# A graph network of four parts on one core: slots of nodes by a scatter beside the node network, out-degrees counted beside the attention

## The chip, the core and the metric

One of the eight cores of a Trainium2 chip runs the whole program in one launch. The metric is the device time in microseconds from start to end of an execution. A core has TensorE (PE, with weight loads PEld), VectorE (DVE), ScalarE (ACT), GpSimd (POOL) and SyncE (SP); SP and GpSimd issue transfers, and 16 DMA engines carry them out.

## The reference, cut to what matters

The input is x (50000 nodes x 128), and 25000 edges (src, dst) sorted by dst. Four networks follow one another, each wrapped as `x = layernorm(x + network(x))`: SAGE with three layers (mean over incoming edges), an attention network with two attention layers and a mean, a network (below "jk") with four layers, and a GCN with three layers.

```python
# the third network: where the degrees are used
deg_out = segment_sum(ones, src, num_segments=n)
deg_in = segment_sum(ones, dst, num_segments=n)
norm_src = rsqrt(maximum(deg_out, 1.0))
norm_dst = rsqrt(maximum(deg_in, 1.0))
for i in range(N_LAYERS):
    m = h * norm_src
    agg = segment_sum(m[src], dst, num_segments=n)
    h = agg * norm_dst
    ...
```

All four networks read `h[src]`, the present value of an edge's source node.

## The kernel before

**Slots.** Only a node that is the dst of some edge gets messages. The edges, padded to 25088 (`SLOTS`), lie as slots in 49 groups (`EG`) of 512, four sub-tiles of 128 each, 196 sub-tiles (`ET`) in all. The last slot of a run of equal dst holds that node's values; other slots hold partial sums. All 50176 (`NODES_PAD`) nodes, 98 groups (`NG`) of 512, are also computed as if they had no incoming edge. A DRAM table holds slots first and the lonely nodes behind, so an edge's source is either "slot s" or "`SLOTS` + node". This number per edge is the `idx` of every later gather. `goes_on` is a mask of bytes, one per slot: same dst as the slot before. `node_mask` marks the nodes without a slot. `l2_weight` is norm_src times norm_dst per edge.

**Blocks.** The program is a row of blocks; each ends with the wait for its stores, and a barrier of all engines. In order: setup; the node network of SAGE (`node_net_block`, here sage_nodes); `maps_block`; sage0 (`slot_hidden_block`), `meta_block`, sage1, `sage_end_block`; `fetch_block`; softmax1, gat1 (`attend_block`), ln1, second, softmax2, gat2, ln2; `mean_block`; `jk_start_block`, four jk layers, jk_end; the node network of the GCN, and three blocks of its slots. Inside a block each engine has its own program; `run_groups` steps over the groups and calls stages with a lag each, in the order of the list, and `wait_for` waits for a semaphore of a group. That order is fixed when the kernel is built; there is no planner.

**Node network of SAGE.** For 98 groups, SP loads x (line 813), TensorE turns it and runs three layers, ScalarE copies and applies ReLU, VectorE adds x and normalizes (lines 700 to 717, 1023 to 1056), SP stores h1, h2, x2 and u. Beside it, GpSimd gathers for the 49 edge groups the x rows of src and dst (`stash`, line 615, 2 x 196 indirect transfers of 128 rows) and writes them to tables of their own (`put`, line 882). At the end GpSimd zeroes `x_in` and `x_again` (lines 888 and 890) for the last, partial group, which SP waits for.

**maps_block.** SP loads dst of each group, repeated over the partitions (`near`, line 527). VectorE compares it with itself shifted by one (`goes_on`, line 573). For each of 196 sub-tiles VectorE makes five one-hot tiles in bf16 (lines 582 to 586): low nine bits and high bits of src and dst, the last two times the slot's tile number and place. TensorE adds three products of them up in PSUM over all sub-tiles (line 554): the count of edges per source, and tile and place of the last slot per destination. VectorE combines these into two numbers a node (out-degree, place), stored as the DRAM table `meta`, and `node_mask` is made.

**sage0 and meta_block.** In sage0 the first SAGE layer of the slots is computed from the stashed rows; beside it, GpSimd gathers the two numbers of `meta` for the source of every edge (`SmallGather`, a ring of five buffers, VectorE copies each into `src_meta`). meta_block makes `idx`, `idx_y`, `idx_jk` and `l2_weight` of them (lines 668 to 676).

**fetch, softmax, gat.** fetch_block is only 196 gathers of GpSimd (line 644). A softmax block is a chain of short operations of VectorE, with TensorE and ScalarE between. In gat, ScalarE weights the fetched rows, VectorE scans and adds (lines 1559 to 1570), GpSimd scales each group's own rows (line 1520).

**Indirect transfers.** GpSimd's transfers are indirect ones: one instruction takes 128 row numbers from a column in SBUF.

The functions that the diff touches:

## Time and profile before

| | us |
|---|---|
| runs shown: median (lowest, highest) | 7210.41 (7204.28, 7210.70) |
| the profiled execution's own time | 7209.73 |
| its span, first to last instruction | 7207.8 |
| PE / PEld / DVE / ACT / POOL busy | 5032.8 / 3367.5 / 4784.7 / 3062.6 / 3388.1 |
| maps_block, first transfer to the next block's first | 1104.96 to 1373.91 |

The mean granted clock of TensorE is 0.801 of its full 2.4 GHz. "Busy" is the time in which an engine had an instruction under way; an idle time is shown in brackets with what ended it. A share near 1 of one engine in a stretch says that this engine sets the pace there. A DMA share of 1 means that all 16 engines had packets under way.

### The profile page before, as it was taken

Reading aid. Unit: us, or ns where it says so; the run is one execution under the profiler, and the core shown is the slowest. Engines: PE = TensorE matmul, PEld = TensorE weight load, DVE = VectorE, ACT = ScalarE, POOL = GpSimd, SP = SyncE. Lnnn points to the kernel's source line nnn. Section 1 sums busy time; section 2 is a strip of 40 time slices with the busy share of each in tenths; the row PEclk is TensorE's granted clock in tenths of the full one; section 3 lists DMA queues with packets and bytes.
Section 4 is the critical chain, followed back from the end, with each engine's and each line's share of the span. In section 5 each row is a group of like instructions: output and inputs, shape, how many; then the busy total and the mean of one; then the engine's idle time right before and its main releaser. Section 6 shows DMA issues by size and latency. Waiting matters only on the chain. (4 is left out here: it accounts for less than half of the span.)

```text
span 7207.8 us, 88239 instructions
## 1 busy us (share of the span) xinstructions
PE 5032.8 (70%) x24324; PEld 3367.5 (47%) x24324; DVE 4784.7 (66%) x14503; ACT 3062.6 (42%) x6979; POOL 3388.1 (47%) x3407
## 2 busy tenths in 40 slices
PE   7999995798989920697435555444489998679221
PEld 5777771364558810596323232221156665456111
DVE  5888789733347612888885566677878886655454
ACT  4666660263333300654444444336756554346000
POOL 5666000274434454373567666673300001765677
PEclk9999999999998955597557667665589999889555
DMA  5888551496766621696445698757856665766332
GB/s 194 277 276 277 214 198 61 126 305 226 245 205 203 195 67 35 175 350 212 140 137 148 129 136 131 122 100 219 270 197 222 222 223 199 209 203 194 95 93 82
DMA packets 1093011, 1317.61 MB, mean 183 GB/s; under 512 B 110351, under 2 KB 791999, under 8 KB 1086254
## 3 DMA queue, kind: packets, MB, share of 16 engines
q1 hardware_dynamic: 974926, 1058.13, 44.3%
q0 software_dynamic: 117600, 253.84, 17.3%
q8 instruction: 203, 3.33, 0.2%
q14 instruction: 282, 2.31, 0.1%
HBM read 633.42 MB, written 682.00 MB: 183 GB/s over the span
## 5 line engine op out<-in xcount | busy, mean ns | idle before, releaser
L615 POOL DMA_INDIRECT jk_layer_msg<-jk,idx_jk x588 | 591.5, 1006 | 268.2 <-issue 174.0
L615 POOL DMA_INDIRECT gcn_msg<-x,idx x196 | 186.9, 954 | 898.0 <-POOLq L137 838.6
L1148 PE MATMUL jk_layer_sum_ps<-ident,jk_layer_weighted 128*128 128x128 f32 x784 | 185.5, 380 | 540.5 <-ACT jk_layer_weighted L1114 540.5
L1148 PEld LDWEIGHTS jk_layer_sum_ps<-ident,jk_layer_weighted 128*128 128x128 f32 x784 | 118.6, 188 | 660.2 <-ACT jk_layer_weighted L1114 660.2
L742 PE MATMUL gcn_nodes_h_ps<-gcn_nodes_h_t,w_gcn 128*128 128x512 f32 x784 | 352.7, 593 | 0.0
L742 PE MATMUL sage_nodes_h_ps<-sage_nodes_h_t,w_ws 128*128 128x512 f32 x784 | 352.5, 592 | 0.0
L1282 DVE COPY sage_h<-sage_turn 128x512 f32<-128x512 f32 x98 | 67.7, 691 | 417.3 <-PE sage_turn L733 417.3
L615 POOL DMA_INDIRECT sage_small_rows<-meta,src_node x196 | 185.0, 944 | 324.2 <-POOLq L137 264.8
L962 ACT ACTIVATE sage_nodes_h_t<-sage_nodes_h_ps,w_b_c 128x512 f32<-128x512 f32 x392 | 247.8, 683 | 198.8 <-PE sage_nodes_h_ps L742 198.8
L2185 PE MATMUL gcn_end_sum_ps<-ident,gcn_end_rows 128*128 128x128 f32 x196 | 54.6, 434 | 389.4 <-DVE gcn_end_rows L2178 389.4
L615 POOL DMA_INDIRECT sage_end_msg<-h,idx x196 | 197.0, 1005 | 270.2 <-ACT sage_end_weighted L1114 159.5
L742 PE MATMUL jk_layer_h_ps<-jk_layer_sum_t,w_jk_w 128*128 128x512 f32 x392 | 321.3, 916 | 0.8 <-DVE jk_layer_sum_t L1170 0.6
L1170 DVE TENSOR_TENSOR_SCAN jk_layer_sum_t<-goes_on,jk_layer_sum_t,jk_layer_sum_ps 128x512 f32<-128x512 uint8 x196 | 249.8, 1274 | 90.2 <-PE jk_layer_sum_ps L1148 90.2
L1950 ACT ACTIVATE jk_layer_h_t<-jk_layer_h_ps,w_jk_b 128x512 f32<-128x512 f32 x196 | 134.7, 687 | 401.9 <-PE jk_layer_h_ps L742 350.0
L962 ACT ACTIVATE gcn_nodes_h_t<-gcn_nodes_h_ps,w_gcn_b_c 128x512 f32<-128x512 f32 x392 | 245.9, 677 | 122.5 <-PE gcn_nodes_h_ps L742 122.5
L1114 ACT ACTIVATE sage_weighted<-sage_msg,inv_deg 128x128 f32<-128x128 f32 (+1 forms) x392 | 146.5, 451 | 353.9 <-DMA sage_msg<-x_msg 336.7
L615 POOL DMA_INDIRECT sage_msg<-h,idx x196 | 185.3, 945 | 230.0 <-ACT sage_weighted L1114 152.2
L742 PE MATMUL sage_h_ps<-sage_sum_t,w_wn 128*128 128x512 f32 x588 | 287.5, 598 | 2.1 <-issue 2.1
L742 PE MATMUL sage_h_ps<-sage_own_t,w_ws 128*128 128x512 f32 x588 | 284.4, 592 | 0.0
L615 POOL DMA_INDIRECT sage_nodes_fetched<-in_x,src_x x196 | 201.5, 1028 | 109.1 <-issue 59.5
L1263 ACT ACTIVATE sage_h_t<-sage_h_ps,w_b_c 128x512 f32<-128x512 f32 x196 | 124.1, 684 | 292.7 <-PE sage_h_ps L742 292.5
L615 POOL DMA_INDIRECT gcn_msg<-r,idx x196 | 201.7, 1029 | 96.6 <-issue 55.4
(481 smaller groups left out, 15979.2 us busy)
## 6 DMA issues: line engine op xcount, KB each, us to landing
h<-sage_nodes_h SPq DMA_DIRECT2D x196, 512.0 KB
h_t<-sage_h_t SPq DMA_DIRECT2D x98, 512.0 KB
h<-sage_h SPq DMA_DIRECT2D x98, 512.0 KB, 3.6
jk_t<-jk_layer_h_t SPq DMA_DIRECT2D x196, 256.0 KB
jk_end_layers<-jk_t SPq DMA_DIRECT2D x49, 1024.0 KB, 5.3
r<-gcn_nodes_h SPq DMA_DIRECT2D x98, 512.0 KB
second_x_in<-u SPq DMA_DIRECT2D x147, 260.0 KB
jk<-jk_layer_h SPq DMA_DIRECT2D x147, 256.0 KB, 4.5
```

The costliest lines, as they stand in the source:

```text
L615: pool.indirect_dma_start(out=into[:, g.number % depth, s, :], out_offset=None, in_=table, in_offset=bass.IndirectOffsetOnAxis(ap=index_ti ...
L742: mm = pe.matmul(ps[:, c, :], w[:, k, c * P:(c + 1) * P], x[:, k, :], start=n == 0, stop=n == len(terms) - 1)
L962: ins = act.activation(tile[:, g.b, c, :], ps[:, c, :], ACT.Relu, bias=bias[:, c:c + 1])
L1114: ins = act.activation(self.weighted[:, g.b, s, :], self.rows_of(g)[:, s, :], self.func, scale=self.weights[0][:, cols(g, SUB, s, 1)])
L1148: mm = pe.transpose(ps[:, c, at_s], self.weighted[:, g.b, s, c * P:(c + 1) * P], self.K.ident[:])
L1170: dve.tensor_tensor_scan(self.sum_t[:, g.b, c, :], self.K.goes_on[:, cols(g, GROUP)], self.ps[g.b][:, c, :], self.sum_t[:, 1 - g.b, c, GRO ...
L1263: ins = act.activation(h_t[:, g.b, c, :], h_ps[:, c, :], ACT.Relu, bias=bias[:, c:c + 1])
L1282: dve.tensor_copy(h[:, g.b, 2:4, :], turn_ps[1][:]).then_inc(out_b.sem, 1)
L1950: act.activation(h_t[:, g.b, 0, :], h_ps[g.b][:, 0, :], ACT.Relu, bias=W.jk_b[:, i:i + 1]).then_inc(kept.sem, 1)
L2185: mm = pe.transpose(self.ps[g.b][:, c, s * P:(s + 1) * P], self.rows[:, g.b, s, c * P:(c + 1) * P], self.K.ident[:])
```

## The change

**Place of a node by a scatter.** maps_block is gone. In setup GpSimd makes `slot_no` (slot s of partition p and sub-tile t: 128 t + p). In the node network of SAGE GpSimd first makes the default places `SLOTS` + node (an iota), SP stores them as the DRAM table `place` before its first load, and after the stash GpSimd issues 196 indirect scatters of one 4-byte number per partition, slot number to row dst, where `idx_out` sends every slot that is not the last of its run out of bounds. GpSimd waits for all of them before it zeroes `x_in` and `x_again`. The `near` loads are in SP's stages of the node network (lag 6), the masks in VectorE's (lag 7), for the first 49 groups. In sage0 GpSimd gathers `place` for each source straight into `K.place`, without a ring and without copies on VectorE. `places_block` takes the place of meta_block: it makes the index tiles and, from a load of the whole table with four numbers a piece, `node_mask`.

**Out-degrees.** `SourceCounts` makes the one-hot tiles of src in fetch_block, two compares and one matmul per sub-tile, and stores the counts. `CountFetch` gathers the count of each edge's source: 42 sub-tiles in softmax1, 66 in gat1, 20 in softmax2, 68 in gat2. `l2_weight` is made in jk_start_block. Five weight tensors (`lin`, three of the GCN, `jk_w`) are loaded in mean_block and not in setup; setup no longer turns dst's high and low parts.

```diff
 # setup: gpsimd
+        link(pool.iota(iota_i[:], pattern=[[1, GROUP]], base=-RJ, channel_multiplier=0))
+        link(pool.tensor_copy(K.lo_iota[:], iota_i[:]))
...
+        link(pool.iota(K.slot_no[:], pattern=[[P, ET]], base=0, channel_multiplier=1))
 # setup: vector
-        for who, tile in (("src", src_i), ("dst", dst_i)):
-            dve.tensor_single_scalar(hi_i[:], tile[:], 9, op=ALU.logical_shift_right)
...
+        dve.tensor_single_scalar(hi_i[:], src_i[:], 9, op=ALU.logical_shift_right)
...
-def maps_block(nc, K, tables):
...
+class SourceCounts:
+    def __init__(self, ph, K, table):
+        self.lo_hot, self.hi_hot = ph.sb("lo_hot", [P, 2, GROUP], BF16), ph.sb("hi_hot", [P, 2, P], BF16)
...
+    def vector_hot(self, dve, t):
+        wait_for(dve, self.hot_used, Group(t - 2))
+        dve.tensor_scalar(self.lo_hot[:, t % 2, :], self.K.lo_iota[:], self.K.src_lo[:, t:t + 1], None, ALU.is_equal)
+        dve.tensor_scalar(self.hi_hot[:, t % 2, :], self.K.hi_iota[:], self.K.src_hi[:, t:t + 1], None, ALU.is_equal).then_inc(self.hot_ready.sem, 1)
+    def tensor_count(self, pe, t):
+        wait_for(pe, self.hot_ready, Group(t))
+        pe.matmul(self.ps[:], self.hi_hot[:, t % 2, :], self.lo_hot[:, t % 2, :], start=t == 0, stop=t == ET - 1).then_inc(self.hot_used.sem, 1)
...
+class CountFetch:
+    def pool_part(self, pool, step=0, steps=1):
+        n = self.end - self.first
+        for t in range(self.first + n * step // steps, self.first + n * (step + 1) // steps):
+            pool.indirect_dma_start(out=self.K.src_count[:, t:t + 1], out_offset=None, in_=self.table,
+                                    in_offset=bass.IndirectOffsetOnAxis(ap=self.K.src_node[:, t:t + 1], axis=0)).then_inc(self.arrived, 16)
+    def pool_wait(self, pool):
+        pool.wait_ge(self.arrived, 16 * (self.end - self.first))
...
 # fetch_block
+        for t in range(ET):
+            counts.vector_hot(dve, t)
+        counts.vector_keep(dve)
...
 # places_block, in place of meta_block
+            sp.dma_start(node_place[:], tables["place"].rearrange("(g p s) k -> p g (s k)", p=P, s=SUB)).then_inc(loaded, 16)
...
+        dve.wait_ge(loaded, 16)
+        link(dve.tensor_copy(node_where[:], node_place[:]))
+        link(dve.tensor_scalar(K.node_mask[:], node_where[:], float(SLOTS), None, ALU.is_ge))
+        link(dve.scalar_tensor_tensor(K.node_mask[:], node_where[:], float(SLOTS + N_NODES), K.node_mask[:], ALU.is_lt, ALU.mult))
...
 # node network of SAGE: sync
+            sp.wait_ge(nodes_ready, 1)
+            sp.dma_start(tables["place"].rearrange("(p c) k -> p (c k)", p=P), node_no[:]).then_inc(places_set, 16)
+            stages = [(load, -1), (load_near, 6), (reload, 3), (store_h1, 3), (store_h2, 4), (store_u, 7), (store_y, 6)]
 # gpsimd
+            pool.iota(node_no[:], pattern=[[1, NODES_PAD // P]], base=SLOTS, channel_multiplier=NODES_PAD // P).then_inc(nodes_ready, 1)
             run_groups(pool, EG, [(put, 1), (stash, 0)])
+            pool.wait_ge(places_set, 16)
+            for t in range(ET):
+                pool.indirect_dma_start(out=tables["place"], out_offset=bass.IndirectOffsetOnAxis(ap=K.idx_out[:, t:t + 1], axis=0),
+                                        in_=K.slot_no[:, t:t + 1], in_offset=None, bounds_check=N_NODES - 1, oob_is_err=False).then_inc(places_done, 16)
+            pool.wait_ge(places_done, 16 * ET)
 # vector
+            stages = [(residual, 4), (apply, 5), (second, 5), (apply2, 6), (count_u, 6), (masks, 7)]
...
 # sage0: gpsimd
+            for t in range(ET):
+                pool.indirect_dma_start(out=K.place[:, t:t + 1], out_offset=None, in_=tables["place"],
+                                        in_offset=bass.IndirectOffsetOnAxis(ap=K.src_node[:, t:t + 1], axis=0)).then_inc(places_in, 16)
+            pool.wait_ge(places_in, 16 * ET)
...
 # gat: gpsimd
-        run_groups(pool, EG, [(scale_own, 0)])
+        run_groups(pool, EG, [(scale_own, 0), (lambda g: fetch.pool_part(pool, g.number, EG), 0)])
+        fetch.pool_wait(pool)
...
 # mean_block: sync
+        for k in LATE_MATRICES:
+            sp.dma_start(W.m[k], A[MATRICES[k][0]].rearrange("(c p) n -> p c n", p=P)).then_inc(weights_in, 16)
+        sp.dma_start(W.jk_w[:], A["L2_gnn_Ws"].rearrange("l p n -> p l n")).then_inc(weights_in, 16)
...
 # jk_start_block: vector
+        dve.tensor_scalar(K.l2_weight[:], K.src_count[:], 1.0, None, ALU.max).then_inc(to_root, 1)
...
 # the order
-            maps_block(nc, K, tables)
...
+            places_block(nc, K, tables)
...
+            fetch_block(nc, "fetch", K, tables["u"][0:V_ROWS], kept, tables["counts"])
+            softmax_block(nc, "softmax1", K, scores, 2, tables["counts"], 0, 42)
+            attend_block(nc, "gat1", K, tables, kept, 42, 108)
...
+            softmax_block(nc, "softmax2", K, scores, 1, tables["counts"], 108, 128)
+            attend_block(nc, "gat2", K, tables, kept, 128, ET)
```

## Rows read from the trace of the kernel before

**Rows 1.** Windows by stage: us, busy us of PE, PEld, DVE, ACT, POOL, PEclk, DMA share, GB/s

```profile
360.00:540.00 180.00, 180.00 (x1028) 128.36 (x1028) 145.21 (x590) 113.48 (x244) 123.77 (x129) 1.00 0.81 277
...
1105.00:1374.00 269.00, 164.29 (x592) 42.51 (x592) 260.56 (x1048) 0.00 (x0) 4.12 (x10) 0.96 0.16 50
...
1400.00:1500.00 100.00, 100.00 (x461) 61.91 (x460) 37.07 (x57) 66.93 (x156) 75.61 (x81) 1.00 1.01 306
...
3400.00:3470.00 70.00, 51.17 (x208) 40.76 (x208) 69.11 (x158) 33.22 (x104) 27.04 (x26) 0.50 0.71 198
```

**Rows 2.** The timeline: start us, us, engine; first transfers of maps and of sage0

```profile
1104.96 6.90 SPq L527 DMA_DIRECT2D maps_near<-dst_pad  x3
...
1373.91 0.37 SPq L1103 DMA_DIRECT2D sage_msg<-x_msg  x1
```

**Rows 3.** The groups of instructions between 1105 and 1374 us: xcount | busy, mean ns

```profile
L582 DVE TENSOR_SCALAR maps_lo_hot<-maps_lo_iota,src_lo 128x512 bf16<-128x512 bf16 x196 | 65.6, 335 | 0.5 <-PE maps_place_ps L554 0.4
...
L584 DVE TENSOR_SCALAR maps_hi_hot<-maps_hi_iota,src_hi 128x128 bf16<-128x128 bf16 x196 | 46.3, 236 | 0.0
...
L573 DVE TENSOR_TENSOR goes_on<-maps_near 128x512 uint8<-128x512 int32 x49 | 33.0, 674 | 0.0
```

**Rows 4.** The timeline of VectorE in setup, one turned column

```profile
42.10 0.43 DVE L480 COPY dst_hi<-setup_turn 128x98 f32<-128x98 f32 x2 [0.35 <-PE setup_turn L421]
```

**Rows 5.** The timeline of VectorE in the node network, one period apart

```profile
899.67 0.69 DVE L1023 TENSOR_TENSOR sage_nodes_y<-sage_nodes_bank_y,w_b 128x512 f32<-128x512 f32 x1 [1.67 <-PE sage_nodes_bank_y L751]
...
910.12 0.69 DVE L1023 TENSOR_TENSOR sage_nodes_y<-sage_nodes_bank_y,w_b 128x512 f32<-128x512 f32 x1 [1.67 <-PE sage_nodes_bank_y L751]
```

**Rows 6.** The timelines of GpSimd, SP and TensorE near the end of the node network

```profile
739.72 0.79 POOL L882 DMA_DIRECT2D x_own<-sage_nodes_fetched  x1 [2.98 <-DMA sage_nodes_fetched<-in_x,dst_x]
...
1033.16 0.35 SPq L810 DMA_DIRECT2D sage_nodes_x_in<-in_x  x1
...
1048.86 0.60 PE L725 MATMUL sage_nodes_bank_x<-ident,sage_nodes_x_in 128*128 128x128 f32 x4
```

**Rows 7.** The groups, and the source view of line 2349: the scatter into out

```profile
L2349 POOL DMA_INDIRECT out<-gcn_end_z,idx_out x196 | 208.3, 1063 | 61.1 <-issue 50.6 <-DVE gcn_end_z L717 10.2 <-DMA out<-gcn_end_z,idx_out 0.3
...
DMA to landing us min/median/max: 2.1/2.2/3.8
```

**Rows 8.** The timeline at the end of sage0 and the start and end of meta

```profile
1618.12 0.94 POOL L615 DMA_INDIRECT sage_small_rows<-meta,src_node  x1 [0.30 <-issue]
...
1644.32 0.26 DVE L668 TENSOR_SCALAR l_weight<-src_meta 128x196 f32<-128x196 f32 x1 [5.00 <-PEq L137]
...
1647.18 0.36 DVE L676 TENSOR_TENSOR l_weight<-l_weight,norm_dst 128x196 f32<-128x196 f32 x1
```

**Rows 9.** The windows view in setup, and the page's part 3

```profile
27.50:28.00 0.50, 0.12 (x1) 0.00 (x0) 0.34 (x1) 0.00 (x0) 0.00 (x0) 1.00 0.77 6
...
q1 hardware_dynamic: 974926, 1058.13, 44.3%
```

**Rows 10.** The groups: gathers of the fetch and beside the node network

```profile
L644 POOL DMA_INDIRECT kept<-u,idx x196 | 184.9, 943 | 131.8 <-PEq L135 72.4 <-issue 59.4
...
L615 POOL DMA_INDIRECT sage_nodes_fetched<-in_x,src_x x196 | 201.5, 1028 | 109.1 <-issue 59.5 <-POOLq L137 49.7
```

**Rows 11.** The timelines of VectorE and GpSimd around one gather

```profile
405.04 0.67 DVE L1053 TENSOR_TENSOR sage_nodes_u<-sage_nodes_u,w_gat_b 128x512 f32<-128x512 f32 x1
...
405.33 1.27 POOL L615 DMA_INDIRECT sage_nodes_fetched<-in_x,src_x  x1 [0.30 <-issue]
```

**Rows 12.** The timeline of softmax1, first and last work

```profile
2828.33 0.27 PEld L1423 LDWEIGHTS softmax_into<-ident,kept 128*98 128x98 f32 x2 [260.21 <-issue]
...
2883.48 0.43 DVE L1478 COPY alpha_self<-softmax_outof 128x98 f32<-128x98 f32 x2 [0.35 <-PE softmax_outof L1432]
```

**Rows 13.** The timeline of VectorE in gat2, one group apart

```profile
3436.68 1.26 DVE L1559 TENSOR_TENSOR_SCAN gat_sum_t<-goes_on,gat_sum_t,gat_sum_ps 128x512 f32<-128x512 uint8 x1
...
3439.34 1.26 DVE L1559 TENSOR_TENSOR_SCAN gat_sum_t<-goes_on,gat_sum_t,gat_sum_ps 128x512 f32<-128x512 uint8 x1
```

More of the change, by code:

```diff
@@ L303, in __init__ @@
         beside = {"gat1": 4, "gat2": 2}
-        self.wide = {k: sb(k, [P, rows // P, cols + beside.get(k, 0)])[:] for k, (_, rows, cols) in MATRICES.items() if k not in SAGE_MATRICES}
+        self.wide = {k: sb(k, [P, rows // P, cols + beside.get(k, 0)])[:] for k, (_, rows, cols) in MATRICES.items() if k not in SAGE_MATRICES + LATE_MATRICES}
         self.m = {k: self.wide[k][:, :, 0:MATRICES[k][2]] for k in self.wide}
@@ L862, in store_u, with load_near @@
             sp.dma_start(at(node_rows(tables["u"], SLOTS), g), u[:, g.b]).then_inc(u_stored.of(g), 16)
+        def load_near(g):
+            if g.number < EG:
+                wait_for(sp, near_used, g.lag(2))
+                sp.dma_start(near[:, g.b, :], tables["dst"][cols(g, GROUP, 0, GROUP + 2)].partition_broadcast(P)).then_inc(near_in.of(g), 16)
         if sage:
-            stages = [(load, -1), (reload, 3), (store_h1, 3), (store_h2, 4), (store_u, 7), (store_y, 6)]
+            sp.wait_ge(nodes_ready, 1)
+            sp.dma_start(tables["place"].rearrange("(p c) k -> p (c k)", p=P), node_no[:]).then_inc(places_set, 16)
+            stages = [(load, -1), (load_near, 6), (reload, 3), (store_h1, 3), (store_h2, 4), (store_u, 7), (store_y, 6)]
         else:
@@ L1058, in _, with masks @@
         if sage:
-            stages = [(residual, 4), (apply, 5), (second, 5), (apply2, 6), (count_u, 6)]
+            def masks(g):
+                if g.number < EG:
+                    wait_for(dve, near_in, g)
+                    now = near[:, g.b, :]
+                    dve.tensor_tensor(K.goes_on[:, cols(g, GROUP)], now[:, 1:GROUP + 1], now[:, 0:GROUP], ALU.is_equal).then_inc(near_used.sem, 1)
+            stages = [(residual, 4), (apply, 5), (second, 5), (apply2, 6), (count_u, 6), (masks, 7)]
         else:
@@ L1187, in slot_hidden_block @@
         own, own_arrived, own_turned = ph.sb("own_rows", [P, 2, SUB, D]), A_("own_arrived"), S("own_turned")
-        small = SmallGather(ph, tables["meta"], 2, K.src_node, src_meta)
+        places_in = ph.sem("places_in")
         own_ps = ph.ps("own_ps", [P, GROUP])
@@ L1223, in _ @@
     def _(pool):
-        fetch = small.pool_fetch if first else sums.pool_fetch
-        run_groups(pool, EG, [(lambda g: fetch(pool, g), 0)])
+        if first:
+            for t in range(ET):
+                pool.indirect_dma_start(out=K.place[:, t:t + 1], out_offset=None, in_=tables["place"],
+                                        in_offset=bass.IndirectOffsetOnAxis(ap=K.src_node[:, t:t + 1], axis=0)).then_inc(places_in, 16)
+            pool.wait_ge(places_in, 16 * ET)
+        else:
+            run_groups(pool, EG, [(lambda g: sums.pool_fetch(pool, g), 0)])
     @block.tensor
@@ L1283, in _ @@
         stages = [(lambda g: sums.vector_carry(dve, g, [made]), 0), (out, 2)]
-        if first:
-            stages.append((lambda g: small.vector_keep(dve, g), 0))
         run_groups(dve, EG, stages)
@@ L1395, in sage_end_block, with softmax_block @@
     ph.close()
-def softmax_block(nc, name, K, source_scores, heads):
+def softmax_block(nc, name, K, source_scores, heads, counts_table, first, end):
     ph = Phase(nc, name, 0)
@@ L1411, in softmax_block, with _ @@
     seg = Segments(ph, K, heads * per_head)
+    fetch = CountFetch(ph, K, counts_table, first, end)
     block = ph.block()
+    @block.gpsimd
+    def _(pool):
+        fetch.pool_part(pool)
+        fetch.pool_wait(pool)
     @block.tensor
@@ L1499, in attend_block @@
     zeroed = ph.sem("zeroed")
+    fetch = CountFetch(ph, K, tables["counts"], first_count, end_count)
     block = ph.block()
@@ L1869, in _ @@
         dve.tensor_copy(row[:], row_ps[:]).then_inc(copied, 1)
+        dve.wait_ge(root, 1)
+        link(dve.reciprocal(K.l2_weight[:], K.l2_weight[:]))
+        link(dve.tensor_tensor(K.l2_weight[:], K.l2_weight[:], K.norm_dst[:], ALU.mult))
     @block.tensor
@@ L2392, in resnorm_gnn @@
     both = SLOTS + NODES_PAD
-    tables = {"dst": dram("dst_pad", SLOTS + 16, 0, I32), "meta": dram("meta", NODES_PAD, 2)}
+    tables = {"dst": dram("dst_pad", SLOTS + 16, 0, I32), "place": dram("place", NODES_PAD, 1, I32), "counts": dram("counts", NODES_PAD, 1)}
     for name, width in (("h1", HID), ("h2", HID), ("x2", D), ("x3", D), ("r1", HID), ("y2", D)):
```

234 lines of the change are left out of this document (83 added, 151 removed).

## The prediction

> **What bounds the kernel now.** I read the page first, for its 40 slices: no engine bounds the whole span, and the busiest one changes with the block. The program is a series of blocks with a barrier between them, so each has a limit of its own and what counts is the wall time of each. The windows give that [rows 1]: the node network runs with TensorE busy all the time (180 of 180 us); the slot-number block (maps, 1105 to 1374) with VectorE busy 260.56 of 269 us and the DMA engines at 0.16; the next block (sage0) with the DMA share at 1.01; the attention blocks (gat) with VectorE busy 69.11 of 70 us. Then the timelines at the edges of the blocks, for who starts and ends them. The block that is taken out is serial: its first transfer is issued at 1104.96, the first of the next block at 1373.91 [rows 2].
>
> **What goes.** The maps block is 1373.91 - 1104.96 = 268.95 us of wall time, and nothing else runs beside it. Its content, 196 sub-tiles of five VectorE compares (236 to 335 ns each) and 49 masks of 674 ns [rows 3], is partly done elsewhere, so each piece is priced where it lands. In setup two of ten turned columns go, each a pair of copies of 0.43 us a pair behind a transpose that keeps VectorE waiting 0.35 us, 0.78 us in all, and four short casts and shifts for dst, which I take at 0.26 us each; all stand on VectorE's chain: -2.6 us [rows 4]. The added iotas there run on GpSimd, which has nothing else: 0.
>
> **Masks beside the node network.** 49 masks of 0.67 us, one per period. A period is 10.46 us (the L1023 rows at 899.67 and 910.12), VectorE waits 1.67 us in each for TensorE [rows 5], so a mask fits and about 1.0 us stays; without that cover it would be 33 us. SP's near load waits for the mask two groups earlier, that is until VectorE ends its step, some 2.3 us later than the norm that SP waited for; behind it on SP stand the reload and the stores of the same step, which have a period to spare, while the next input load stands ahead of it. The near loads bring DMA work: in the maps window 0.16 x 269 / 49 = 0.88 us of all engines for each, so in a 10.46 us period the share rises from 0.81 to 0.89 during the first 49 groups. TensorE is not waiting for loads there; sage0 shows where it ends, at 1.01 [rows 1]. I take 0, and up to 15 us for the range. At the start SP waits for a GpSimd iota of 392 numbers a partition (nearest, a GpSimd operation on 512: 1.04 us [rows 1], 27.04 us for 26) and issues one store: between 0.5 and 1.5, +0.9 us.
>
> **The scatter.** GpSimd's last put is at 739.72; then it waits, with nothing to do but zero two tiles near the end [rows 6]. The nearest row for a scatter is L2349: mean 1.063 us, and 0.30 us of issue before each, with 2.2 us from issue to landing [rows 7]. 196 x 1.36 = 267 us; from 741 that ends near 1010, with the masks lengthening some gathers near 1020. The zeroing of x_in now comes behind it; SP asks for it only at 1033.16, after a store, and TensorE turns that group at 1048.86 with a load of about 3 us between [rows 6]: the scatter may last until about 1045 at no cost. So it is hidden, with 25 us to spare; it costs 1 us for each us past that, from a price of about 1.55 us a scatter on. The page "DMA: Bandwidth & Descriptors" of the Trainium skill (Specifications) says that below 512 B the DMA engines read, modify and write; no row here has a 4-byte write to DRAM. It gives no price, and the sum does not use it.
>
> **Places.** The gathers of slot numbers in sage0 are as many as the small gathers before, of which the last was issued at 1618.12, 26 us before the next block's first instruction [rows 8]; fewer waits change nothing. Sage0 begins on a TensorE left half cold by the tail: +1 us. Then meta's chain of 3.2 us (1644.32 to 1647.54) [rows 8] gives way to a load of 392 places per partition in pieces of 16 bytes: 128 x 98 = 12,544 packets. The nearest row is a stretch of setup with 4-byte packets: 6 GB/s x 0.5 us = 3 KB = 750 packets at a share of 0.77 [rows 9], hence some 8.4 us at 1500 packets per us, plus 2 us to land. The other end is the mean over all hardware queues, 0.443 x 7207.8 x 16 / 974926 = 52 ns of one engine for a packet of 1.1 KB: 784 packets on each engine would then take 41 us [rows 9]. I take 10.5 us, being a row of small packets, plus 1.4 us of conversions: +9 us net (from +5 to +40).
>
> **Counting beside the fetch.** Per tile VectorE has 335 + 236 ns and TensorE one of the three matmuls [rows 3]; with two buffers and the hand-overs about 0.53 us a tile, 104 us in all, inside a block set by 196 gathers of 0.943 + 0.30 us, 244 us [rows 10]. What can cost is GpSimd slowed by VectorE. With VectorE idle these gathers take 943 ns; beside the node network the first kind takes 1028 ns, and a single one started 0.29 us into a two-input VectorE operation of 0.67 us takes 1.27 us [rows 10, 11]. Of about 80 gathers in 104 us I lengthen each by 0.1 us: +8 us; between 0 and 0.3 us each (+24). The Trainium skill's "SBUF — State Buffer" (A bandwidth-pool intuition that's wrong) says that a VectorE operation in a two-port mode, or with two SBUF inputs, holds the port pair that GpSimd writes descriptors through, and GpSimd waits until it ends. The single gather above agrees; by the rule in its full strength, the bf16 compares holding GpSimd off through the 104 us, this step would cost about 100 us, and the page's case makes it a rival.
>
> **Count gathers beside the attention.** Softmax1: 42 x 1.35 = 56.7 + 2 to land = 59 us, in a block whose chain runs from 2828.33 to 2883.91, 55.6 us [rows 12]: +4 us (0 to 11). Softmax2: 20 x 1.35 + 2 = 29 us beside a chain of about 28 us: +2 us (0 to 5). Gat1: GpSimd has 27.04 / 26 = 1.04 us of own rows per group and waits the rest; a group lasts 2.67 us (3436.68 to 3439.34) [rows 1, 13]. With 66/49 gathers of 1.25 us it gets 1.04 + 1.68 = 2.72 us, 3 us more over 49 groups than VectorE: +3 us with the landing. Gat2: 1.04 + 68/49 x 1.25 = 2.77 us, +0.10 x 49 = 5 us, of which buffers give some back and the landing takes some: +6 us. Here GpSimd takes VectorE's place as the bound by a hair; at 1.0 us a gather another 4 us each.
>
> **Mean and jk_start.** Five weight loads stand before the first input load on SP (2.4 us), but the first gathers land later; the square root and reciprocal run beside the stores of jk_start. Together +1 us.
>
> **Sum**, made against the profiled execution (span 7207.8, own time 7209.73; the median of the runs shown is 7210.41, 0.7 above): -268.95 - 2.6 + 0.9 + 1 + 9 + 8 + 4 + 2 + 3 + 6 + 1 = -236.7 us; 7209.7 - 236.7 = 6973.
>
> **The rivals.**
> (A) As summed, GpSimd's added queue stays under its covers: 6973; own range 6955 to 6995.
> (B) GpSimd becomes the bound in five places, because gathers beside VectorE take 1.55 us with their issue, as the 1.27 us row has it. Fetch +24, softmax1 +11, softmax2 +5, gat1 (1.04 + 1.347 x 1.55 = 3.13 against 2.67) +23, gat2 (3.19) +26; with the other +11.9 that is 101, and -271.6 + 101 = -170.6: 7039. For it: the single rows; against it: most gathers beside VectorE are not lengthened, since the mean is 1028 ns and not 1270 [rows 10].
> (C) The port lock at full strength in the fetch alone: +100 in place of +8, 7065. Against it: the same mean, taken beside eight tensor_scalar operations in each period.
> (D) The added work costs almost nothing: places +5, the start and the half-cold clock +2: -271.6 + 7 = -264.6, so 6945.
> (E) Slower: the scatters of single words are slow. If each takes p, the node network ends 741 + 196 p - 1045 late. The gain of 237 is gone at p = 2.76 us, and at 3.0 us the time is 6973 + 284 = 7257. For it: writes of 4 bytes, of which no row exists; against it: with 512-byte rows the same form takes 1.06 us and lands in 2.2 [rows 7].
> (F) The block is not really removed from the path, since sage0 would wait for something else of it: nothing in sage0 reads more than goes_on and the two tables written by 741 us, so I give this next to nothing.
>
> **Numbers.** A 0.60, B 0.14, C 0.04, D 0.18, E 0.02, others 0.02. Range 6940 to 7040: A and D whole, and B up to its centre. About 0.2% (14 us) is what a measurement of this kernel can tell from no change; faster 0.97, same 0.01, slower 0.02.
>
> **What would show it.** In the trace of after: the first instruction of sage0 near 1104; node-network periods still 10.46 us with VectorE's wait shrunk to about 1.0 us; the 196 scatters between 741 and 1020 and x_in's zeroing behind them before 1045; 10 to 12 us between the places load and its conversion; fetch gathers above 944 ns in the first 104 us and at 944 after; gat periods of 2.7 to 2.8 us, with GpSimd without idle time. The forecast is wrong if the node network ends after 1110, if the places load takes over 30 us, or if the gat blocks last over 10 us longer than before.

## The result, and the profile of the changed kernel

The changed kernel takes 6985.21 us (median of 4 runs, 6975.1 to 6986.7) against 7207.34 us before (median of 4, 7197.51 to 7210.70): ratio 0.9691, 95% interval 0.9674 to 0.9708. The forecast was 6973, the range 6940 to 7040. The profiled execution has a span of 6984.9 us and an own time of 6986.7, 223.0 less than before; the sum had -236.7. Cut at the same instruction in both traces, the stages are:

| stage, first marked instruction to the next | before | after | change | forecast |
|---|---|---|---|---|
| start to the first x load of the node network | 51.29 | 49.55 | -1.7 | -1.7 |
| node network | 1053.7 | 1076.8 | +23.2 | 0 |
| maps | 268.95 | - | -268.95 | -268.95 |
| sage0 with meta or places | 275.2 | 281.4 | +6.2 | +10 |
| sage1, sage_end | 924.8 | 923.3 | -1.5 | 0 |
| fetch | 254.4 | 264.7 | +10.3 | +8 |
| softmax1 | 56.6 | 60.2 | +3.7 | +4 |
| gat1 | 138.0 | 142.3 | +4.2 | +3 |
| ln1, second, softmax2 | 321.1 | 322.2 | +1.2 | +2 |
| gat2, ln2, mean | 421.7 | 428.2 | +6.4 | +6.5 |
| jk_start to the end | 3442.1 | 3436.2 | -5.9 | +0.5 |

(The forecast's +1 for mean and jk_start is halved over the last two rows. Nothing was changed behind jk_start, and that stretch differs by as much from one trace to another: in the kernels below whose values there are right it lasts 3429 to 3452 us, its last block alone 516 to 531. Stages that no edit touches repeat less well than they look: sage0 with places lasts 283.8 to 285.3 us in e1 to e8, which is +9 to +10, and not 281.4.)

One term is far off, the node network. The windows of the changed kernel (us, busy us of PE, PEld, DVE, ACT, POOL, granted clock, DMA share, GB/s), the first stretch beside the stash (of which [rows 1] has 360 to 540 us before), the others beside the scatters:

```profile
180.00:540.00 360.00, 360.00 (x2061) 257.11 (x2060) 310.77 (x1212) 227.45 (x485) 225.34 (x231) 1.00 0.87 295
810.00:900.00 90.00, 82.40 (x460) 57.74 (x459) 64.06 (x259) 49.91 (x108) 69.58 (x68) 0.98 0.97 177
960.00:1050.00 90.00, 90.00 (x528) 65.24 (x527) 71.75 (x290) 57.15 (x121) 68.99 (x69) 1.00 0.79 191
```

Beside the stash TensorE stays full and the share rises from 0.81 to 0.87 (forecast 0.89). Behind it, where GpSimd only scatters words of 4 bytes, the DMA engines are full (0.97) while they move less than before, and TensorE, which had no idle time in this stretch before, stands still for 7.6 of 90 us. The tiles' views say when the stash and the scatters run (duration min/median/max in ns, first and last start):

```profile
L850 POOL DMA_DIRECT2D x_own<-sage_nodes_fetched x49: 790/795/819, 62.1 to 793.6; - x49
...
L856 POOL DMA_INDIRECT place<-slot_no,idx_out x196: 982/985/1542, 794.7 to 1061.8; - x196
```

The median scatter takes 0.985 + 0.30 us, a little less than forecast; with some longer ones and one pause of 9.2 us, 267.1 us pass from the first start to the last, as forecast. But the last put, at 739.72 before [rows 6], is at 793.6. The scatters end at 1063 us and not at 1010. The waits for transfers between 790 and 1130 us (total us, times, longest):

```profile
DVE sage_nodes_x L1019 <- DMA x<-sage_nodes_x: 22.6, 9, 5.1
DVE sage_nodes_y L1002 <- DMA sage_nodes_x_again<-in_x: 10.8, 1, 10.8
PEld sage_nodes_bank_x L683 <- DMA sage_nodes_x_in<-in_x: 8.6, 1, 8.6
```

The first is VectorE waiting for the stores of x2 to land, so that it may write their buffer again, mostly between 800 and 900; the other two are the end, and the timeline shows their origin:

```profile
1061.85 0.98 POOL L856 DMA_INDIRECT place<-slot_no,idx_out  x1 [0.30 <-issue]
1064.02 0.53 POOL L863 MEMSET sage_nodes_x_in<- 128x512 f32 x1 [1.19 <-DMA place<-slot_no,idx_out]
1064.64 0.35 SPq L772 DMA_DIRECT2D sage_nodes_x_in<-in_x  x1
...
1067.34 1.12 PE L683 MATMUL sage_nodes_bank_x<-ident,sage_nodes_x_in 128*128 128x128 f32 x4 [7.79 <-DMA sage_nodes_x_in<-in_x]
```

SP asks for this load at 1033.16 in the kernel before [rows 6]. Now SP waits for the zeroing first, and everything else in its queue waits behind that load, the reload of x_again among it.

### The profile page after: what moved, and what is told of

It reads as the page before. It is cut to its first block and busy times, and to the rows that moved or that the text cites. A ratio compares the mean times of both kernels' runs of the same rounds, so it can differ in the third digit from the quotient of the medians.

```text
span 6984.9 us, 87340 instructions
## 1 busy us (share of the span) xinstructions
PE 4969.1 (71%) x23920; PEld 3343.0 (48%) x23924; DVE 4656.6 (67%) x13844; ACT 3065.4 (44%) x6979; POOL 3791.6 (54%) x3795
## 5 line engine op out<-in xcount | busy, mean ns | idle before, releaser
L602 POOL DMA_INDIRECT kept<-u,idx x196 | 195.1, 995 | 131.7 <-ACTq L135 72.3
L573 POOL DMA_INDIRECT gcn_end_msg<-y,idx x196 | 187.9, 959 | 108.9 <-issue 59.4
L1094 ACT ACTIVATE jk_layer_weighted<-jk_layer_ready,l_weight 128x128 f32<-128x128 f32 x588 | 186.9, 389 | 136.9 <-DVE jk_layer_ready L1981 136.4
```

What stands on the lines that cost most here:

```text
L573: pool.indirect_dma_start(out=into[:, g.number % depth, s, :], out_offset=None, in_=table, in_offset=bass.IndirectOffsetOnAxis(ap=index_ti ...
L602: pool.indirect_dma_start(out=kept[:, t, :], out_offset=None, in_=table, in_offset=bass.IndirectOffsetOnAxis(ap=K.idx[:, t:t + 1], axis=0) ...
L1094: ins = act.activation(self.weighted[:, g.b, s, :], self.rows_of(g)[:, s, :], self.func, scale=self.weights[0][:, cols(g, SUB, s, 1)])
```

## The experiments

Where a ratio stands, it is to the kernel before on the same chip; stages are cut as in the table.

**Which part of the change costs the 23 us.** One kernel leaves the scatters out, two put something else in their place, and a fourth reorders them. (In the first three all places keep their default, so the values from there on are wrong, and their whole times say nothing here.) e1 drops the loop over line 856 and its wait. e2 and e3:

```
e2: out=tables["wide"] (a new table of 50176 rows x 128), in_=K.ident[:]
e3: out=K.place[:, t:t + 1], in_=tables["place"], in_offset by K.src_node[:, t:t + 1]
```

e4 takes dst once more from its table, 196 consecutive slots to a partition, so that column t holds slots 196 p + t (shortened):

```diff
+  sp.dma_start(wide_dst[:, 0:ET], rows_of_dst)            # and the next slot's dst behind it
+  pool.iota(wide_slot[:], pattern=[[1, ET]], base=0, channel_multiplier=ET)
+  wide_last = (wide_dst[:, 1:] == wide_dst[:, :ET]);  wide_idx = wide_last * 65536 + wide_dst
-  ... IndirectOffsetOnAxis(ap=K.idx_out[:, t:t + 1]), in_=K.slot_no[:, t:t + 1]
+  ... IndirectOffsetOnAxis(ap=wide_idx[:, t:t + 1]), in_=wide_slot[:, t:t + 1]
```

> Leaves out the 196 scatters, so the default places stay in the table (source slots are wrong from there on); the near loads and masks stay. In the changed kernel the node network lasted 1076.9 us from its first x load to the first load of sage0, against 1053.7 before. Theory S (the scatters cost it, by the late zeroing of x_in and by slowing the other transfers): TensorE busy 100 of 100 us between 800 and 900 (92.4 with scatters), DMA share there near 0.55 (0.93), stores of u landing in 3.0 us (7.5), and the stretch 1054 +- 2 us, total about 6963. Rival N (near loads and masks cost it): about 1065 to 1075 us, TensorE still idle between 800 and 900. The stash ends near 794 us by both, since the near loads stay.

> The same 196 scatters to the same row numbers, but each writes a row of 512 bytes (the identity tile) into a table of its own; the places stay at their default. Theory Q (any write of 4 bytes is dear, whatever its neighbours): the DMA share between 810 and 900 falls from 0.97 to 0.55 plus the rows' own bytes (about 0.65), TensorE is busy 90 of 90 us, and the node network lasts 1066 us (the late tail of 11 stays). Theory P (neighbouring words of one stretch of DRAM are written by many engines at once): the same, since the rows are now 512 bytes apart. Rival R (the number of write packets, of whatever size): share 0.9 or more, TensorE idle 7 us as in the changed kernel, 1077 us.

> In the place of the 196 scatters stand 196 gathers of one 4-byte number each from the table of places: as many packets of the same size, but reads. Theories P and Q (writes are what costs): DMA share near 0.58 between 810 and 900, TensorE busy 90 of 90, node network 1066 us. Rival R (small packets as such, or GpSimd's writing of descriptors): share 0.9, 1077 us.

> The same 4-byte scatters of the same values, but in another order: the slots of one scatter are 196 apart (slot 196 p + t) and not neighbours, so their places lie on average 1.6 KB apart in DRAM, where 128 neighbouring slots cover under 2 KB in all, the first ones only a few dozen words. Adds two loads at the start, an iota and three short VectorE operations, some 3 us at most. Theory P (neighbouring words): the share between 810 and 900 falls from 0.97 to near 0.6, stores of u land in about 3 us, TensorE is busy 90 of 90 us, and the node network lasts 1066 to 1069 us, total about 6975. Theory Q (4 bytes as such): nothing changes or it gets worse, since the 23% of slots that write are now in every scatter: 1077 us or more, total 6985 to 6990.

(The 23% in the last one is a wrong figure of mine: counted in the reference's inputs, 17,475 of the 25,088 slots are the last of their run and write.) Measured, node network: e1 1053.8, e2 1062.9, e3 1061.6, e4 1066.7 us. The windows 810 to 900 of e1, e2, e3 and e4, in that order:

```profile
810.00:900.00 90.00, 90.00 (x523) 64.90 (x522) 71.84 (x287) 56.34 (x120) 0.00 (x0) 1.00 0.55 202
```
```profile
810.00:900.00 90.00, 90.00 (x517) 64.28 (x517) 72.07 (x292) 56.49 (x122) 68.97 (x70) 1.00 0.65 229
```
```profile
810.00:900.00 90.00, 90.00 (x523) 64.85 (x522) 71.86 (x286) 56.35 (x120) 68.98 (x69) 1.00 0.56 203
```
```profile
810.00:900.00 90.00, 90.00 (x523) 64.81 (x522) 72.69 (x292) 55.76 (x120) 69.02 (x69) 1.00 0.57 201
```

e1 is the kernel before to a tenth of a microsecond: theory S holds, and the near loads and masks cost this block nothing by themselves (rival N falls). e3 takes rival R with it: the same number of small packets, as reads, leave the share at 0.56 and TensorE full. e4 decides between P and Q: the same 196 scatters, the same 4 bytes, the same values, and the share is 0.57 and TensorE full. So small writes alone are not dear (e4), and neighbouring rows alone are not either (e2, whose 512-byte rows are neighbours too, and which skips the same slots): it takes both, small writes that lie together. How near each other they must be, and why it costs, no run shows. In the original order the 128 words of one scatter lie together. dst is sorted and dense at its low end (in the inputs the slots of tile 0 point to nodes 0 and 1, those of tile 5 to 33 to 47, of tile 190 to 47271 to 47752), and the disturbance fades as the scatters proceed, 0.97 in 810 to 900 and 0.79 in 960 to 1050, though more of the slots write by then. What it does to the rest is in the DMA view, 810 to 900: the changed kernel's own packets from SP's queue keep the engines busy 1.7 times as much for less data (first fence; the second is e4).

```profile
q1 hardware_dynamic: 6446, 15.81, 92.6%
q0 software_dynamic: 2159, 0.04, 3.4%
```
```profile
q1 hardware_dynamic: 7418, 17.90, 54.8%
q0 software_dynamic: 2179, 0.04, 1.8%
```

The scatters' own packets take 3.4%; the price is paid by the stores and loads beside them (207 ns a packet against 106: share x 90 us x 16 / packets). e2, e3 and e4 still lose 8 to 13 us: each lists a wait for x_again of 7 to 12 us at the end. As a whole kernel e4 is at 6975.34 us, ratio 0.9679 (0.9663 to 0.9695); this interval overlaps that of the changed kernel, so only the windows and stages tell the two apart.

**The end of the block.** e5 takes the zeroing away from GpSimd:

```diff
-  wait_for(pool, turned, last.lag(2));  pool.memset(x_in[:, last.b], 0.0)      # and x_again
+  # VectorE's stages: at step 96, and behind residual(95)
+  wait_for(dve, turned, g.lag(1));      dve.memset(x_in[:, (NG - 1) % 2], 0.0)
+  wait_for(dve, y_summed, g);           dve.memset(x_again[:, (NG - 1) % 2], 0.0)
```

> The scatters stay as they are; the zeroing of x_in and x_again for the last group is done by VectorE, one group ahead of its use, and no longer by GpSimd behind the scatters. Theory T (the late end of the scatters costs only by that zeroing, and the slowed transfers cost by themselves): the 10.8 us wait for x_again at the end goes, the 22.6 us of waits for stores of x2 between 800 and 900 stay, and the node network lasts 1066 us from its first x load to sage0's first load (1076.9 in the changed kernel, 1053.7 before and without scatters); total near 6975. Rival: the last load is late for the slow transfers, not for the zeroing: 1073 us or more. Second rival: GpSimd's own end holds the barrier: it ends near 1064, before the last stores near 1105, so no.

1065.3 us; the wait for x_again shrinks to 0.6 us and that for x2 is left:

```profile
DVE sage_nodes_x L1014 <- DMA x<-sage_nodes_x: 22.1, 8, 6.5
```

Against the changed kernel's own trace, 11.5 us are thus the zeroing and 11.7 the slowed transfers. Both shares vary: e7 and e8 below have the changed kernel's node network as it is, and it lasts 1071.3 and 1072.6 us there, with waits for x_again of 3.1 and 8.3 us; without the late zeroing 11.7 to 16.7 us are left (e5, e6, e9). That there are two parts is shown, their sizes only so far. (One time, 6988.91 us, where the kernel before took 7216.71 on that chip.)

**Why the stash is late.**

```diff
 e6 -  dve.tensor_tensor(K.goes_on[:, cols(g, GROUP)], now[:, 1:GROUP + 1], now[:, 0:GROUP], ALU.is_equal)
    +  dve.memset(K.goes_on[:, cols(g, GROUP)], 0)
 e9 -  near loads and the comparison
    +  setup: goes = same dst as the slot before, as bytes, stored as a table
    +  sp.dma_start(K.goes_on[:, cols(g, GROUP)], tables["goes"][cols(g, GROUP)].partition_broadcast(P))
```

> Keeps the near loads of the node network, but VectorE writes a zero mask (one short memset per group) in place of the comparison of two tiles; results of the segments are wrong for it. In the changed kernel the last put of the stash is issued at 793.6 us, before at 739.7. Theory L (the near loads, 263 KB each through the same DMA engines, hold up the stash's gathers): 788 to 794, GpSimd still waiting about 2.9 us a group for the fetched rows, DMA share 0.87 in 180 to 540. Rival M (VectorE's two-input comparison keeps GpSimd from its descriptors): 740 to 750, GpSimd's waits back near 2.0 us a group.

> The masks goes_on are made once in setup (as bytes, two short copies and one store more) and loaded repeated, 64 KB a group, in the place of near loads of 263 KB and VectorE's comparison. The stash's last put was issued at 739.7 us before the change, between 785 and 801 in five kernels with near loads and masks, at 779.5 with the loads but without the comparison. Theory L (bytes of the near loads): 745 to 755 us, the DMA share between 180 and 540 back from 0.87 to about 0.83. Rival M (what is left of the delay is not of the loads, but of the order on SP or of the fuller VectorE): 775 or more. The scatters then end near 1010 to 1015, so the zeroing is no longer late, while the slowed transfers stay: node network 1064 to 1066 us.

The last put in e6 and in e9, where the kernels with loads and masks have it between 783.7 and 801.0:

```profile
L850 POOL DMA_DIRECT2D x_own<-sage_nodes_fetched x49: 790/792/822, 61.2 to 779.5; - x49
```
```profile
L855 POOL DMA_DIRECT2D x_own<-sage_nodes_fetched x49: 790/792/857, 62.0 to 756.1; - x49
```

The delay is GpSimd's wait for the fetched rows, which the put needs (line 850; its us and times before, in the changed kernel, in e6 and in e9):

```profile
  DMA sage_nodes_fetched<-in_x,dst_x: 89.0, 47
  DMA sage_nodes_fetched<-in_x,dst_x: 138.2, 47
  DMA sage_nodes_fetched<-in_x,dst_x: 124.4, 47
  DMA sage_nodes_fetched<-in_x,dst_x: 101.1, 47
```

The comparison accounts for some 10 of 50 us (4 to 21, by which of the other traces it is held against), and three quarters of the bytes for another 23; the rest over 740 goes with the quarter that stays or with something else of the change. Against most of the traces the loads are the larger cause; both expectations were missed by little (779.5 against 788 to 794, 756.1 against 745 to 755). e6's node network is 1065.9 (its masks, and with them its values, are wrong), its scatters end at 1048 and the x_again wait is gone, as the forecast's limit of about 1045 has it. e9's is 1070.4 and not 1064 to 1066: with the scatters starting at 757, VectorE waits 26.0 us for x2 from 790 us on, in place of 22.6. So an earlier stash alone does not pay: e9 as a whole is at 6997.36 us (one time), 0.969 of the kernel before, as the changed kernel is.

**GpSimd beside VectorE.** e7 makes the one-hot tiles f32; e8 cuts the 196 count gathers otherwise:

```diff
 e7 -  ph.sb("lo_hot", [P, 2, GROUP], BF16), ph.sb("hi_hot", [P, 2, P], BF16)
    +  ph.sb("lo_hot", [P, 2, GROUP]), ph.sb("hi_hot", [P, 2, P])
 e8 -  softmax1 0:42, gat1 42:108, softmax2 108:128, gat2 128:196, a wait in each
    +  softmax1 0:38, gat1 38:98, ln1 98:107, softmax2 107:125, gat2 125:186, ln2 186:196, one wait in jk_start
```

> The one-hot tiles of fetch_block are f32 in place of bf16 (the iotas stay bf16), nothing else changes. In the changed kernel 98 gathers lie beside the counting at a median of 1046 ns, and two tiles of VectorE and one gather share a period of 1.35 us; after the counting a gather takes 945 ns; the block lasts 264.7 us against 254.4 before. Theory V (the compares in bf16 run in VectorE's fast form, and that form and GpSimd's descriptor writes exclude each other): with f32 out the compare of 512 takes near 0.6 us, gathers beside it stay at 944 to 950 ns, and the block lasts 254 to 256 us if the counting ends within it (0.85 us a tile for VectorE, f32 matmuls at the half clock about 1.7 us a tile, 330 us: then TensorE sets the block at 335 us, and only the gathers' duration decides). Rival W (any VectorE work beside a gather lengthens it): 1046 ns or more.

> Only the places of the 196 count gathers change: softmax1 38 (42), gat1 60 (66), ln1 9 (0), softmax2 18 (20), gat2 61 (68), ln2 10 (0), and one semaphore for all is waited for in jk_start in place of a wait at each block's end. In the changed kernel these cost 3.7 us in softmax1, 4.3 in gat1, 7.1 in gat2 and about 1 in softmax2 against before. Theory G (GpSimd's queue is the bound by a hair and its last gathers hang over): softmax1 back to 56.6 us, gat1 138 to 139, gat2 with ln2 and mean (gat2's first load to jk_start) 421 to 422 in place of 428.2, total -15 us, near 6970. Rival H (GpSimd's descriptor writes slow VectorE in these blocks whatever their number): at most 2 us gained in each gat, total -5.

The gathers of fetch_block while the counting runs and behind it, changed kernel (two windows), then the first stretch of e7 and its compare:

```profile
L602 POOL DMA_INDIRECT kept<-u,idx x98: 987/1046/1058, 2331.1 to 2462.1; - x98
...
L602 POOL DMA_INDIRECT kept<-u,idx x97: 941/945/954, 2464.7 to 2584.7; - x97
```
```profile
L602 POOL DMA_INDIRECT kept<-u,idx x103: 940/948/1170, 2330.0 to 2459.7; - x103
...
L531 DVE TENSOR_SCALAR fetch_lo_hot<-lo_iota,src_lo x196: 480/486/699, 2329.4 to 2528.7; 128x512 f32<-128x512 bf16 x196
```

Theory V holds in what it forecast: the compare is longer (486 against 350 ns) and the gathers are back at 948 at the median, though VectorE is still busy for 0.74 of the stretch (0.79 in the changed kernel). They are not quite free of it: their mean while the counting runs is 966 ns (1045 in the changed kernel, 943 in the kernel before, without any counting), and the block lasts 258.1 us, against 254.4 before. That the form of the compare is what decides is argued from this one change of type. VectorE is delayed by the gathers too: two tiles and one gather keep a common beat of 1.35 us in the changed kernel, every other compare taking 0.49 us and not 0.34, behind a wait for TensorE:

```profile
2400.59 0.49 DVE L531 TENSOR_SCALAR fetch_lo_hot<-lo_iota,src_lo 128x512 bf16<-128x512 bf16 x1 [0.28 <-PE fetch_count_ps L536]
...
2401.16 0.34 DVE L531 TENSOR_SCALAR fetch_lo_hot<-lo_iota,src_lo 128x512 bf16<-128x512 bf16 x1
```

"SBUF — State Buffer" (A bandwidth-pool intuition that's wrong) of the Trainium skill has such a lock between the two engines, under which one of them waits until the other is done; the trace agrees with its direction, and the measured size is 0.10 us a gather, not a standstill. (The recorded prediction adds a VectorE operation with two SBUF inputs; the same page of the Trainium skill has that case under the heading before, and only against a GpSimd operation that reads SBUF, as these gathers read their row numbers.) My fear of 330 us for TensorE was wrong: it got its full clock (granted 1.00 from 2340 us on, where the changed kernel has 0.50) and ended at 2530.

In e8 softmax1 is 56.6 us, gat1 139.2, and from gat2 to jk_start 423.6. Rival H falls; theory G has softmax1 right, but the two gat stretches stay 1 to 2 us above the kernel before. Ratio 0.9661 (0.9645 to 0.9677), which just touches the interval of the changed kernel.

The reason is in the queue instructions at a block's end (line 135). In the changed kernel, behind fetch with 196 gathers, softmax1 with 42, softmax2 with 20 and gat2 with 68 (the first of its pair is the next barrier's, 40 ns):

```profile
L135 POOLq DRAIN  x1: 7077/7077/7077, 2588.0 to 2588.0; - x1
...
L135 POOLq DRAIN  x1: 3478/3478/3478, 2651.8 to 2651.8; - x1
...
L135 POOLq DRAIN  x1: 1682/1682/1682, 3118.1 to 3118.1; - x1
...
L135 POOLq DRAIN  x2: 40/2824/5607, 3258.0 to 3264.3; - x2
```

GpSimd ends each block with a drain, and everyone waits for it. In these blocks it lasts 82 to 84 ns for each gather issued (3478 / 42, 1682 / 20, 5607 / 68), and no more than 7.08 us behind the 196 of fetch. (That is behind a wait for the last landing. In e8, without that wait, the drain starts earlier and takes in the rest of the queue, 18.25 us in softmax1, but ends before VectorE.) What it does in that time no view shows, nor what ends the rise: at the program's end the drain lasts 5.61 us behind 196 gathers and 196 scatters. In gat2 VectorE is done at 3255.17 and the next block starts at 3264.34:

```profile
3254.30 0.87 DVE L1561 BATCH_NORM_STATS2 slot_stats<-gat_rows 128x6 f32<-128x128 f32 x4
3264.34 0.85 DVE L1595 TENSOR_TENSOR ln_work<-node_stats 128x392 f32<-128x392 f32 x1 [9.17 <-PEq L137]
```

That wait was 2.41 us before, where the drain, without gathers, lasted 1.13 us. Of the 9.17 us now, 2.8 are the wait for the last gather to land (the drain starts at 3257.95) and 5.6 the drain. VectorE's own stretch is as long as before: gat1 134.9 us in both, gat2 134.6 against 134.3. e12, below, tests it.

**Together.** e10 holds e4, e5, e7, e8 and one edit more: the load of all places and node_mask move from places_block to fetch_block. e11 adds e9's masks.

> Five edits to the changed kernel together: scatters in spread order, zeroing by VectorE, f32 one-hot tiles in fetch, count gathers spread over six blocks, and the load of all places with node_mask moved from places_block into fetch_block. By stages, against the changed kernel: node network 1055 to 1057 us from its first x load (1076.9; 10 each from the first two, less some 3 for the spread order's loads), sage0 with places 276 us (281 to 285), fetch 258 us (264.7), softmax1 56.6 (60.2), gat1 139 (142.3), gat2 with ln2 and mean 423.6 (428.2). Sum about -48 us: near 6937 where the changed kernel has 6985; ratio to the kernel before 0.962 to 0.964. Rival: the load of places lengthens fetch by its 9 us or the gathers there, and the sum is -38.

> The five edits and the byte masks. If the scatters' end no longer matters once the zeroing is VectorE's, as I think, the byte masks add nothing beyond the five: within 3 us of them, since TensorE sets the node network's pace either way. Rival: the near loads also cost at the start or end of the block, and 3 to 6 us are gained.

e10: 6953.74 us (median of 5) where the kernel before took 7221.48, ratio 0.9623 (0.9610 to 0.9636); e11: 6954.74, ratio 0.9627 (0.9614 to 0.9640). The interval of e10 lies below that of the changed kernel (0.9674 to 0.9708). By stages e10 has node network 1054.5, sage0 with places 276.9, fetch 258.2, softmax1 56.6, gat1 139.3, gat2 to jk_start 424.0: each within 1 us of its expectation, and fetch did not get longer by the load of places (258.1 in e7). By the ratios 0.0068 x 7207 = 49 us are gained on the changed kernel (48 expected); the stages named add up to 44 of it. e11's node network is 1054.2: the byte masks add nothing, because the scatters' end no longer matters.

e12 is e10 with the count gathers of the gat blocks issued so that the drain starts early:

```diff
-  (lambda g: fetch.pool_part(pool, g.number, EG), 0)                # cuts 38, 98, 107, 125, 186
+  (lambda g: fetch.pool_part(pool, g.number, EG - 4) if g.number < EG - 4 else None, 0)   # 40, 99, 108, 127, 187
```

> The five edits, with the count gathers cut 40, 59, 9, 19, 60, 9 and, in the two gat blocks, issued in the first 45 of 49 groups only. Theory D: what a gat block still loses against the kernel before (139.2 to 139.4 us against 138.0, and 1 to 2 us in gat2) is not the gathers but GpSimd's drain at the block's end, which starts behind its last gather and lasts longer the more gathers were issued: in the changed kernel 1.68 us after 20, 3.48 after 42, 5.44 after 66, 5.61 after 68, 7.08 after 196; in the five-edit kernel gat1's drain runs from 2752.2 for 7.5 us and ends 3 us behind VectorE. Ended 8 to 10 us earlier it is covered: gat1 138.0 to 138.6, gat2 to jk_start 421.8 to 422.8, total 2 to 4 us below the five-edit kernel (ratio 0.9618 to 0.9621). Rival G: GpSimd's rate is the bound (45 x 1.06 + 59 x 1.27 = 122.6 us against 45 x 2.67 = 120.2), so the denser queue holds VectorE up: gat1 140 to 142, gat2 to jk_start 425 or more.

```profile
L135 POOLq DRAIN  x2: 5982/8226/10469, 2749.0 to 2761.3; - x2
```

gat1's drain ends at 2755.0 us, 136.0 behind the block's start (2759.7 and 138.4 in e10), gat1 lasts 138.3 us and gat2 to jk_start 421.2, which is the kernel before's own 138.0 and 421.7: theory D holds, and the denser queue costs nothing (rival G). The lengths fit too: 5.98 us here, behind 59 gathers, is what gat1's drain takes in the kernel before without any (1.15 us) plus 82 ns a gather. In the whole time the 3.9 us that these two stages gain on e10 cannot be told: 6955.16 us, ratio 0.9626 (0.9613 to 0.9639), where e10 has 0.9623.

## Why the prediction was right, and where it was not

- **What goes** and **setup**: as summed, -268.95 and -1.7 with the start of the node network.
- **Masks beside the node network**: right for the block. VectorE waits 1.1 us a period (36.0 us in 34 waits, 180 to 540 us) and TensorE is full; without scatters the block takes its 1053.7 us. But the sentence "I take 0" stopped at TensorE. The near loads and masks lengthened a chain beside it, the stash, by 44 to 61 us (54 in the changed kernel), and the next step built on its end. I had "the masks lengthening some gathers near 1020", 10 us for what was 54.
- **The scatter** is the step that failed, worth all of the 23.2 us (e1). Its count and price were right (267 us). Wrong were the start (741, measured 795), with that "hidden, with 25 us to spare": the end came 18 us after 1045, of which 11.5 us were seen in that trace (e5) and 3 and 8 us of waits in e7 and e8. And it asked only for the time of the scatters, not for what they do to the transfers beside them: 11.7 us (to 16.7 in e9), which none of the rivals had, since E prices a scatter for itself. The sentence of "DMA: Bandwidth & Descriptors" (Specifications) of the Trainium skill on transfers below 512 B pointed at a danger, but by size; here, at 4 bytes in both, order alone made the difference (e4), and what a lone 4-byte write costs no run shows.
- **Places**: +6.2 with sage0's start against +10. From the first instruction behind sage0 to sage1's first gather it is +7.0, where +9 was forecast; sage0 itself is 0.8 us shorter than before in this trace and 2 to 3 longer in e1, e4, e7 and e8. The +1 for a TensorE "half cold" at its start has nothing behind it: the granted clock of the first 10 us is 0.55, and it was 0.50 before. The load took 8.9 us from issue to its conversion, against the 10.5 taken from [rows 9]:

```profile
1396.01 0.36 SPq L621 DMA_DIRECT2D places_node_place<-place  x1
...
1404.90 0.37 DVE L632 CAST places_node_where<-places_node_place 128x392 f32<-128x392 int32 x1 [7.56 <-DMA places_node_place<-place]
```

- **Counting beside the fetch**: +10.3 against +8. The lengthening of 0.1 us was right (1046 against 945 ns); it held 98 gathers and not 80, since the counting took 131 us, not 104. The forecast's 0.53 us a tile left out two things: the longer compares, 0.15 us in every second tile, and VectorE's waits for TensorE, 26.7 us in all, whose product takes 0.61 us at the granted clock of 0.50. Rival C, a full standstill, is refuted.
- **Count gathers beside the attention**: +4, +2, +3, +6 against 3.7, 1.2, 4.2 and 6.4 (with mean): right numbers for a wrong reason. "GpSimd takes VectorE's place as the bound by a hair" did not happen, since VectorE's stretches kept their length; the gathers take 988 ns at the median in both gats. The step had the landing of the last gathers ("+3 us with the landing"), but not what stands behind it and is the larger part: GpSimd's drain at the block's end (e12). Rival B is refuted with it. The same drain was there before, behind fetch: 7.08 us of the 8 from its last landing to softmax1's first instruction.
- **The numbers**: 6973 against 6985.2, inside the range and just inside A's own (6955 to 6995), and part of that is luck. The 23.2 us that were missed would alone have given 6996; they are offset by places (4 us, in this trace alone) and by 7 us in stages that the change leaves alone.

## What to carry to other kernels

"Hidden" has two questions: does the added work end before it is asked for, and does what it shares (DMA engines, ports) still serve those on the path; add up every delay of the chain that feeds it. Issue tiny scatters so that the words of one instruction lie far apart (here 1.6 KB on average). Put what the last step of a block needs (here a zeroing) on an engine that is not at the end of a long queue, and stop filler work on GpSimd early enough for its drain to be covered.

## What the runs showed of the hardware

- 4-byte scatters to neighbouring words raise the mean DMA time of the packets in SP's queue from 106 to 207 ns and store landings with it (u: 3.0 us at the median in e1, 14.8 in the changed kernel, 810 to 900); the same scatters 196 slots apart do not, nor do scatters of neighbouring 512-byte rows (share 0.65, TensorE full).
- A likely case for reads was not sought: with all places at their default (e1, e2, e3) every gather of three jk layers reads one and the same row, and the stretch from jk_start to the GCN's slots takes 2630, 2629 and 2622 us against 2322 (the whole kernels 7273, 7287 and 7273 us, one time each). That the one row is the cause was not tested. In e1 (second fence) the share is higher and the traffic lower than in the changed kernel (first):

```profile
3900.00:4000.00 100.00, 50.85 (x154) 29.41 (x152) 62.30 (x109) 38.20 (x96) 72.71 (x73) 0.62 0.93 132
```
```profile
3900.00:4000.00 100.00, 42.06 (x130) 24.62 (x130) 51.27 (x91) 31.80 (x79) 53.63 (x52) 0.64 0.99 105
```

  In the real kernels, too, every source without a slot is sent to this row (16,290 of the 25,000 edges, counted in the inputs); whether copies of it would pay was not tried.
- GpSimd's drain at the end of a block lasts about 82 ns per gather issued in it, seen from 20 to 68 gathers; behind the 196 of fetch it is 7.08 us, in the kernel before too.
- The counting's f32 product of 128 x 512 takes two instructions of 0.59 us a tile, the second started before the first ends, and the bf16 product one of 0.61 us. The first kept TensorE busy (195 of 200 us) at a granted clock of 1.00, the second (about 0.75 of the time) had 0.50, and a tile took 1.02 us in e7 against 0.67 in the changed kernel.
